# One signal for each unit of eight matmuls instead of one for each matmul, in a GNN kernel of gather passes

## The chip, the cores and the metric

The kernel runs on one core of a Trainium2 chip. Its five engines (TensorE or PE for matmuls, VectorE or DVE, ScalarE or ACT, GpSimd or POOL, SyncE or SP) run programs of their own and meet only at semaphores: an instruction can add to a semaphore when it is finished, and an engine can wait until a semaphore has reached a count. The metric is the time of one execution on the device in microseconds, the median of several timed runs. Beside these there is one execution under the hardware profiler, which is where all rows come from.

## The reference

Four graph networks run one after the other on 4096 nodes with 256 features and 65,536 edges (`src`, `dst`, sorted by `dst`), with a layer norm after each. All of them gather the rows of the source nodes, change them per edge, and add them up by destination node:

```
# layer of the first network, five times
emsg = relu(h_in[src] + edge_attr @ We[l] + be[l])
agg  = segment_sum(emsg, dst)
h    = mlp(h_in + agg) ... + h_in
# second: x[src] * edge_weight, segment_sum
# third:  attention; segment_max over dst of the scores, then
#         segment_sum of exp(score - max) * h[src]
# fourth: h[src] * norm, segment_sum, three times
```

`dst` is the floor of 4096 times the square of a uniform number. Of the 32 blocks of 128 nodes block b therefore ends at about the share sqrt((b+1)/32) of the edges: the first blocks have many edges each, the last about a thousand.

## The kernel before

There are eleven passes over the edges. Nine are made by `edge_pass`: five of kind MESSAGE (first network), one WEIGHTED (second), three PLAIN (fourth). `max_pass` finds the segment maximum, `attend_pass` does the attention sum and isn't touched. Between them stand node phases of dense matmuls.

A pass goes over 64 **octets** of eight tiles of 128 edges (U = 8). For each tile POOL issues one indirect DMA (L262), which gathers 128 rows into a slot of `ring`. The ring holds four octets (OB = 4): POOL begins octet h when PE has given octet h-4 free (`octet_free`) and ACT has copied its indices (`idx_ready`).

The sum by destination is a matmul. For an octet and a block of 128 destination nodes, a **unit**, DVE writes eight 128x128 one-hot matrices into `S` (`one_hots`, L235, two instructions of four matrices each, here called g0 and g1), and PE multiplies the eight of them with the eight ring tiles and adds up in `psA` (L331). An octet has as many units as blocks that its edges touch: one or two. With 32 blocks cut into 64 octets this makes 95 units in a pass; 31 octets have two, 7 of them in the first half of the pass, 24 in the second, and 14 of these among the last 16 octets.

`S` and `psA` exist once. In one unit DVE writes g0, which waits for the first four matmuls of the unit before (`onehot_used`, `c + 4 * g + 4`), then waits for all eight of them, adds `psA` to `AGG` (L373, `unit_added`), and writes g1. PE waits for `unit_added` before the first matmul and for `onehot_ready` before the first and the fifth. At the end of an octet's units PE reads the next count of units from `span_row`, which costs its sequencer a load and some register work.

MESSAGE passes have edge features besides. `encode` (L301) makes eight small bf16 matmuls for the next octet into `psE`, two at a time, each pair behind the DVE additions that have read the pair's bank (`pre_added`). DVE adds `psE` to the gathered rows (L388), ACT applies the relu (L347, `message`). PE does at each octet: encode for the next octet, then the load of the count, then the units. The stacked features come in by a DMA of SP, which waits until `encoded` counts the whole octet.

The max pass takes two octets at a time, a **group** of 16 gathers (L428). PE turns the scores (L440, L441, then `scoresT`), DVE scans them, PE turns them back, and the units follow (L457, 128x9), with `merge_last` (L492, L495 and on) in the place of the sum. POOL may begin group n+2 when `scoresT` has counted group n.

Of the kernel before, what the change touches and what calls it, by code (L numbers as in the profile page):

```python
# [22 lines left out]
U = 8  # L23
NO = NT // U
OB = 4
# [15 lines left out]
def build(nc, x, src, dst, edge_attr, edge_weight, vn_emb0, We, be, W1, b1, W2, b2, bn_g, bn_b, bn_m, bn_v,  # L41
# [3 lines left out]
    with ctx:  # L45
# [35 lines left out]
        we_stk = sb("we_stk", [P, D], BF16)  # L81
# [45 lines left out]
        picks = sb("picks", [P, MT, HEADS + 1])  # L127
# [16 lines left out]
        octet_free = sem("octet_free")  # L144
# [121 lines left out]
        def edge_pass(kind, k, l=0, loads=None, first_work=None, first_dve=None):  # L266
            with nc.Block() as block:
# [20 lines left out]
                @block.tensor  # L288
                def _(pe):
                    if first_work:  # L290
                        first_work[0](pe)
                    def encode(i, ob):

                        o = NO * l + OB * i + ob

                        pe.wait_ge(stk_in[ob], 16 * (NG * l + i + 1))
                        for u in range(U):
                            if u % 2 == 0:

                                pe.wait_ge(pre_added, U * o + u + 2)  # L300
                            nc.tensor.matmul(psE[:, D * u:D * u + D], stk[:, ob, P * u:P * u + P],  # L301
                                             we_stk[:, :], start=True, stop=True).then_inc(encoded, 1)

                    if kind == MESSAGE:
                        encode(0, 0)
                    with pe.Fori(0, NG) as i:
                        for ob in range(OB):
                            h = OB * i + ob
                            if kind == MESSAGE:

                                if ob < OB - 1:
                                    encode(i, ob + 1)
                                else:
                                    with pe.If(i < NG - 1):
                                        encode(i + 1, 0)
                            cnt = pe.value_load(span_row[0:1, bass.ds(2 * h + 1, 1)], min_val=1, max_val=NB)

                            def unit(_, first):
                                c = pe.snap(npe)

                                pe.wait_ge(unit_added, c + 2 * U)
                                for u in range(U):
                                    q = U * ob + u
                                    if first:
                                        if kind in (MESSAGE, WEIGHTED):
                                            pe.wait_ge(message, NT * k + U * h + u + 1)
                                        else:
                                            pe.wait_ge(gathered[q], 16 * (NG * k + i + 1))
                                    if u % 4 == 0:
                                        pe.wait_ge(onehot_ready, c + u + 4)  # L330
                                    nc.tensor.matmul(psA[:, 0:D], S[:, u, :], ring[:, q, 0:D],  # L331
                                                     start=(u == 0), stop=(u == U - 1)).then_inc(onehot_used, 1)
                                pe.reg_add(npe, npe, U)

                            units(pe, None, cnt, unit)
                            pe.drain().then_inc(octet_free, 1)

                @block.scalar
                def _(act):
# [16 lines left out]
                @block.vector  # L356
                def _(dve):
                    nc.vector.memset(AGG[:, :], 0.0)

                    nc.vector.memset(psA[:, 0:D], 0.0)  # L360
                    dve.reg_mov(last_blk, 0)
                    dve.drain()
                    if first_work:
                        first_work[2](dve)
                    if first_dve:
                        first_dve(dve)

                    def add_sums():

                        b = nc.s_assert_within(dve.snap(last_blk), 0, NB - 1,  # L370
                                               skip_runtime_bounds_check_because="a unit's block")
                        a = AGG[:, bass.ds(b * AW, D)]
                        return nc.vector.tensor_tensor(a, a, psA[:, 0:D], ALU.add)  # L373

                    with dve.Fori(0, NG) as i:
                        for ob in range(OB):
                            h = OB * i + ob
                            o = NO * l + h
                            lo, cnt = span_of(dve, h)

                            def messages():
                                for u in range(U):
                                    q = U * ob + u
                                    dve.wait_ge(gathered[q], 16 * (NG * k + i + 1))
                                    if u % 2 == 0:

                                        dve.wait_ge(encoded, U * o + u + 2 + OB * U)
                                    nc.vector.tensor_tensor(ring[:, q, 0:D], ring[:, q, 0:D],  # L388
                                                            psE[:, D * u:D * u + D], ALU.add).then_inc(pre_added, 1)

                            def unit(blk, first):
                                c = dve.snap(nd)
                                if first and kind == MESSAGE:
                                    messages()
                                one_hots(dve, h, blk, c, 0)

                                dve.wait_ge(onehot_used, c + U)
                                dve.wait_ge(unit_added, c + U)
                                add_sums().then_inc(unit_added, U)
                                one_hots(dve, h, blk, c, 1)  # L400
                                dve.reg_mov(last_blk, blk)
                                dve.reg_add(nd, nd, U)

                            units(dve, lo, cnt, unit)
                    c = dve.snap(nd)
                    dve.wait_ge(onehot_used, c + U)
                    dve.wait_ge(unit_added, c + U)
                    add_sums()
# [7 lines left out]
        def max_pass(k):  # L416
            with nc.Block() as block:
# [14 lines left out]
                @block.tensor  # L432
                def _(pe):
                    with pe.Fori(0, NG) as i:
                        for g in range(GR):
                            n = GR * i + g
                            for q in range(MT * g, MT * g + MT):
                                pe.wait_ge(gathered[q], 16 * (NG * k + i + 1))
                            pe.wait_ge(d16_ready, n + 1)
                            nc.tensor.transpose(psE[:, 0:P], gs[:, P * g:P * g + P], ident[:, :])  # L440
                            nc.tensor.transpose(psE[:, 512:512 + P], d16[:, :], ident[:, :]).then_inc(scoresT, 1)  # L441
                            pe.wait_ge(runs_ready, n + 1)
                            nc.tensor.transpose(psE[:, 1024:1024 + P], run[:, :], ident[:, :])
                            nc.tensor.transpose(psE[:, 1536:1536 + P], last[:, :], ident[:, :]).then_inc(runsT, 1)
                            pe.wait_ge(picks_ready, n + 1)
                            for half in range(2):
                                cnt = pe.value_load(span_row[0:1, bass.ds(2 * (2 * n + half) + 1, 1)],
                                                    min_val=1, max_val=NB)

                                def unit(_, first):  # L450
                                    c = pe.snap(npe)

                                    pe.wait_ge(unit_added, c + 2 * U)
                                    for u in range(U):
                                        if u % 4 == 0:
                                            pe.wait_ge(onehot_ready, c + u + 4)
                                        nc.tensor.matmul(psA[:, (HEADS + 1) * u:(HEADS + 1) * (u + 1)], S[:, u, :],  # L457
                                                         picks[:, U * half + u, :], start=True, stop=True
                                                         ).then_inc(onehot_used, 1)
                                    pe.reg_add(npe, npe, U)  # L460

                                units(pe, None, cnt, unit)
                                pe.drain().then_inc(octet_free, 1)

                @block.scalar
                def _(act):
# [1310 lines left out]
```

## Time and profile before

| | us |
|---|---|
| median of three timed runs | 9055.8 |
| lowest and highest of them | 9051.29, 9059.39 |
| the profiled execution, first to last instruction | 11096.4 |
| PE busy in it | 6221.1 (56%) |
| POOL busy in it | 5936.1 (53%) |
| DVE busy in it | 4228.8 (38%) |

The profiled execution took 2040.6 us more than the median of the timed ones, so its rows can't be added up to the time without asking which of them are there only under the profiler.
### The profile page before, as it was taken

All of it is one profiled execution on the core that took longest, in us unless ns stands there. A gap on an engine that the chain in (4) does not pass through costs nothing. (4 is left out here: it accounts for less than half of the span.)

```text
span 11096.4 us, 128036 instructions
## 1 busy us (share of the span) xinstructions
PE 6221.1 (56%) x27247; PEld 4898.8 (44%) x27248; DVE 4228.8 (38%) x9200; ACT 1828.6 (16%) x5238; POOL 5936.1 (53%) x5947
## 2 busy tenths in 40 slices
PE   3557655855575566557456434445663555456454
PEld 2445544634464455446344323434452344344343
DVE  5344444443443444434122723344453223124123
ACT  3222222222122222213332100001110000000000
POOL 2654465365536545652665365545545655655665
PEclk9789888978887888889788755567876788778787
DMA  4332333133323323332322000022222222222222
GB/s 148 106 97 79 93 102 90 56 115 99 89 67 106 94 77 92 104 91 67 90 83 72 19 3 2 2 55 72 72 55 73 85 78 77 85 76 72 85 87 71
DMA packets 424174, 855.04 MB, mean 77 GB/s; under 512 B 142497, under 2 KB 206754, under 8 KB 424098
## 3 DMA queue, kind: packets, MB, share of 16 engines
q0 software_dynamic: 263184, 679.84, 21.6%
q1 hardware_dynamic: 160914, 174.39, 5.2%
q8 instruction: 23, 0.38, 0.0%
q14 instruction: 53, 0.43, 0.0%
HBM read 790.64 MB, written 63.18 MB: 77 GB/s over the span
## 5 line engine op out<-in xcount | busy, mean ns | idle before, releaser
L262 POOL DMA_INDIRECT ring<-node_table,idx x4608 | 4557.0, 989 | 3214.9 <-issue 1615.9
L331 PE MATMUL psAT<-ring,S 128*128 128x256 f32 x13680 | 3792.2, 439 | 2375.5 <-DVE AGG L373 1330.1
L331 PEld LDWEIGHTS psAT<-ring,S 128*128 128x128 f32 x13680 | 2973.7, 223 | 3158.7 <-issue 1702.0
L235 DVE SCALAR_TENSOR_TENSOR S<-iota,block_start,dst_f 128x512 f32<-128x512 f32 x1900 | 1423.6, 749 | 3122.1 <-remote 1598.4
L347 ACT ACTIVATE ring<-ring 128x256 f32<-128x256 f32 x2560 | 885.8, 416 | 3282.4 <-DVE ring L388 2302.8
L388 DVE TENSOR_TENSOR ring<-ring,psE 128x256 f32<-128x256 f32 x2560 | 888.0, 416 | 399.5 <-remote 214.9
L373 DVE TENSOR_TENSOR AGG<-AGG,psAT 128x256 f32 x864 | 363.6, 421 | 1624.6 <-remote 1005.5
L301 PE MATMUL psE<-we_stk,stk 128*128 128x256 bf16 x2560 | 420.8, 318 | 963.6 <-issue 883.8
L262 POOL DMA_INDIRECT ring<-att_table,idx x512 | 513.3, 1003 | 491.4 <-issue 228.1
L301 PEld LDWEIGHTS psE<-we_stk,stk 128*128 128x128 bf16 x2560 | 254.8, 110 | 1147.6 <-issue 997.8
L428 POOL DMA_INDIRECT gs<-score_table,idx x512 | 508.9, 994 | 370.9 <-PE psE L441 214.8
L246 ACT COPY idx<-src_i 128x8 int32 x704 | 138.7, 197 | 3299.6 <-DMA ring<-node_table,idx 2352.7
L457 PE MATMUL psAT<-picks,S 128*128 128x9 f32 x1520 | 340.0, 363 | 309.5 <-DVE cand L495 197.0
L457 PEld LDWEIGHTS psAT<-picks,S 128*128 128x128 f32 x1520 | 331.4, 330 | 327.9 <-issue 201.5
L1428 POOL TENSOR_TENSOR tab<-H,be_row 128x256 f32<-128x256 f32 x128 | 105.9, 827 | 500.3 <-DVE H L1425 500.3
L351 ACT ACTIVATE ring<-ring,weight 128x256 f32<-128x256 f32 x512 | 259.0, 507 | 526.6 <-DMA ring<-node_table,idx 477.7
L952 PE MATMUL psE<-tT,w_sb 128*128 128x128 f32 x2560 | 315.3, 277 | 0.9 <-ACT tT L981 0.8
L952 PEld LDWEIGHTS psE<-tT,w_sb 128*128 128x128 f32 x2560 | 301.7, 193 | 2.4 <-ACT tT L981 2.1
L965 PE MATMUL psE<-w_sb,hT 128*128 128x256 f32 x1280 | 301.9, 379 | 0.0
L965 PEld LDWEIGHTS psE<-w_sb,hT 128*128 128x128 f32 x1280 | 231.4, 190 | 25.0
L990 ACT ACTIVATE hT<-psE,b_col 128x128 f32<-128x128 f32 x640 | 182.5, 368 | 228.8 <-PE psE L952 228.8
L939 PE MATMUL psAT<-ident,tin 128*128 128x128 f32 x320 | 67.2, 293 | 219.3 <-DVE tin L199 184.9
(268 smaller groups left out, 4359.6 us busy)
## 6 DMA issues: line engine op xcount, KB each, us to landing
stk<-stack_table SPq DMA_DIRECT2D x320, 256.0 KB
ring<-node_table,idx POOLq DMA_INDIRECT x4608
node_table<-tab SPq DMA_DIRECT2D x224, 128.0 KB, 1.7
stack_table<-stk SPq DMA_DIRECT2D x64, 256.0 KB, 2.0
gs<-score_table,idx POOLq DMA_INDIRECT x512
ring<-att_table,idx POOLq DMA_INDIRECT x512
w_sb<-in_L_gnn_W SPq DMA_DIRECT2D x10, 512.0 KB
att_table<-tab SPq DMA_DIRECT2D x32, 132.0 KB, 1.8
```

Source lines behind the costliest of these rows:

```text
L235: nc.vector.scalar_tensor_tensor(S[:, 4 * g:4 * g + 4, :], iota[:, :].unsqueeze(1).to_broadcast([P, 4, P]), block_start[:, bass.ds(blk, 1) ...
L262: nc.gpsimd.indirect_dma_start(ring[:, q, 0:gw], None, table, bass.IndirectOffsetOnAxis(ap=idx[:, q:q + 1], axis=0)).then_inc(gathered[q], 16)
L301: nc.tensor.matmul(psE[:, D * u:D * u + D], stk[:, ob, P * u:P * u + P], we_stk[:, :], start=True, stop=True).then_inc(encoded, 1)
L331: nc.tensor.matmul(psA[:, 0:D], S[:, u, :], ring[:, q, 0:D], start=(u == 0), stop=(u == U - 1)).then_inc(onehot_used, 1)
L347: nc.scalar.activation(ring[:, q, 0:D], ring[:, q, 0:D], ACT.Relu).then_inc(message, 1)
L351: nc.scalar.activation(ring[:, q, 0:D], ring[:, q, 0:D], ACT.Copy, scale=weight[:, bass.ds(RING * i + q, 1)]).then_inc(message, 1)
L373: return nc.vector.tensor_tensor(a, a, psA[:, 0:D], ALU.add)
L388: nc.vector.tensor_tensor(ring[:, q, 0:D], ring[:, q, 0:D], psE[:, D * u:D * u + D], ALU.add).then_inc(pre_added, 1)
L428: nc.gpsimd.indirect_dma_start(gs[:, HEADS * q:HEADS * q + HEADS], None, score_table, bass.IndirectOffsetOnAxis(ap=idx[:, q:q + 1], axis=0 ...
L457: nc.tensor.matmul(psA[:, (HEADS + 1) * u:(HEADS + 1) * (u + 1)], S[:, u, :], picks[:, U * half + u, :], start=True, stop=True).then_inc(o ...
L952: ins = nc.tensor.matmul(psE[:, 512 * q + P * j:512 * q + P * j + P], w1_sb[:, f, P * j:P * j + P], tT[:, q, P * f:P * f + P], start=(f == ...
L965: ins = nc.tensor.matmul(result_of(q), a, w, start=(n == 0), stop=(n == len(terms) - 1))
```

## The change

The matmuls of `encode` (L301), of the units of `edge_pass` (L331) and of the units of `max_pass` (L457) lose their increments. After each eight of them PE executes a drain, which ends when all matmuls before it are finished and adds 8 to the same semaphore. The drain that signalled `octet_free` at the end of an octet becomes a plain increment. In `messages()` DVE waits once for all eight encodings, not pair by pair. The counts of all semaphores at the end of a unit are as before, and no instruction changes its place in an engine's program; the waits on DVE are the same text, but `onehot_used` now rises by eight at once where it rose one by one, so that the wait of g0 for "the first four of the unit before" is now a wait for all eight and the drain.

```
-                                             we_stk[:, :], start=True, stop=True).then_inc(encoded, 1)
+                                             we_stk[:, :], start=True, stop=True)
+                        pe.drain().then_inc(encoded, U)
...
-                                                     start=(u == 0), stop=(u == U - 1)).then_inc(onehot_used, 1)
+                                                     start=(u == 0), stop=(u == U - 1))
+                                pe.drain().then_inc(onehot_used, U)
                                 pe.reg_add(npe, npe, U)
 
                             units(pe, None, cnt, unit)
-                            pe.drain().then_inc(octet_free, 1)
+                            pe.sem_inc(octet_free, 1)
...
-                                    if u % 2 == 0:
-
-                                        dve.wait_ge(encoded, U * o + u + 2 + OB * U)
+                                    if u == 0:
+
+                                        dve.wait_ge(encoded, U * o + U + OB * U)
...
-                                                         picks[:, U * half + u, :], start=True, stop=True
-                                                         ).then_inc(onehot_used, 1)
+                                                         picks[:, U * half + u, :], start=True, stop=True)
+                                    pe.drain().then_inc(onehot_used, U)
                                     pe.reg_add(npe, npe, U)
 
                                 units(pe, None, cnt, unit)
-                                pe.drain().then_inc(octet_free, 1)
+                                pe.sem_inc(octet_free, 1)
```

## Rows read from the trace of the kernel before

**Rows 1.** The page: span, engines, the gather group (busy, mean ns | idle).
```profile
span 11096.4 us, 128036 instructions
...
PE 6221.1 (56%) x27247; PEld 4898.8 (44%) x27248; DVE 4228.8 (38%) x9200; ACT 1828.6 (16%) x5238; POOL 5936.1 (53%) x5947
...
L262 POOL DMA_INDIRECT ring<-node_table,idx x4608 | 4557.0, 989 | 3214.9 <-issue 1615.9
```

**Rows 2.** Waits on POOL (us in total, times, longest).
```profile
POOL ring L262 <- PEq L336: 1497.1, 314, 26.1
...
POOL ring L262 <- ACT idx L246: 291.7, 62, 16.9
POOL gs L428 <- PE psE L441: 214.8, 29, 14.3
...
POOL ring L262 <- PEq L707: 67.3, 15, 12.4
```

**Rows 3.** Stretches: a MESSAGE pass, the max pass, a PLAIN pass.
```profile
core 0: us, PE busy (x) PEld busy (x) DVE busy (x) ACT busy (x) POOL busy (x), PEclk, DMA share, GB/s
1195.30:2092.20 896.90, 522.47 (x2107) 397.50 (x2105) 369.21 (x826) 189.12 (x579) 504.21 (x512) 0.81 0.33 97
...
6383.40:7308.50 925.10, 383.90 (x1648) 349.86 (x1648) 306.57 (x894) 12.62 (x64) 508.92 (x512) 0.50 0.05 2
...
8425.90:9249.40 823.50, 424.66 (x1520) 331.80 (x1520) 181.53 (x288) 12.63 (x64) 503.19 (x512) 0.79 0.28 82
```

**Rows 4.** Timeline of a PLAIN pass, one unit held up (start us, us, ..., [idle <-releaser]).
```profile
9023.85 3.71 PE L331 MATMUL psAT<-ring,S 128*128 128x256 f32 x16 [1.69 <-issue]
...
9032.67 0.75 DVE L235 SCALAR_TENSOR_TENSOR S<-iota,block_start,dst_f 128x512 f32<-128x512 f32 x1 [8.84 <-remote]
...
9042.50 0.42 DVE L373 TENSOR_TENSOR AGG<-AGG,psAT 128x256 f32 x1 [9.07 <-remote]
```

**Rows 5.** Timeline, end of a PLAIN pass, all gathers landed: three units.
```profile
9231.40 3.72 PE L331 MATMUL psAT<-ring,S 128*128 128x256 f32 x16 [1.26 <-DVE S L235]
9233.55 0.75 DVE L235 SCALAR_TENSOR_TENSOR S<-iota,block_start,dst_f 128x512 f32<-128x512 f32 x1 [2.17 <-PE psAT L331]
9235.27 0.42 DVE L373 TENSOR_TENSOR AGG<-AGG,psAT 128x256 f32 x1 [0.97 <-PE psAT L331]
...
9235.83 3.72 PE L331 MATMUL psAT<-ring,S 128*128 128x256 f32 x16 [0.71 <-DVE AGG L373]
...
9240.77 3.72 PE L331 MATMUL psAT<-ring,S 128*128 128x256 f32 x16 [1.22 <-DVE AGG L373]
```

**Rows 6.** Timeline, matmuls of the same shape without signals, node phase.
```profile
9257.02 1.03 PE L965 MATMUL psE<-wb_sb,tT 128*128 128x256 f32 x4
```

**Rows 7.** Timeline, a MESSAGE pass: one octet of two units, undisturbed.
```profile
4086.18 1.04 PE L301 MATMUL psE<-we_stk,stk 128*128 128x256 bf16 x8 [0.61 <-issue]
...
4087.70 3.71 PE L331 MATMUL psAT<-ring,S 128*128 128x256 f32 x16 [0.48 <-issue]
...
4092.14 3.72 PE L331 MATMUL psAT<-ring,S 128*128 128x256 f32 x16 [0.72 <-issue]
...
4096.11 0.75 DVE L235 SCALAR_TENSOR_TENSOR S<-iota,block_start,dst_f 128x512 f32<-128x512 f32 x1
```

**Rows 8.** Timeline, POOL's gathers in a PLAIN pass.
```profile
10613.12 0.94 POOL L262 DMA_INDIRECT ring<-node_table,idx  x1 [0.30 <-issue]
```

**Rows 9.** Timeline, the max pass: from one pair of transposes to the units.
```profile
7080.72 0.42 PE L441 MATMUL psE<-ident,d 128*128 128x128 f32 x1
...
7087.00 3.58 PE L457 MATMUL psAT<-picks,S 128*128 128x9 f32 x16 [2.57 <-DVE cand L495]
...
7091.27 3.58 PE L457 MATMUL psAT<-picks,S 128*128 128x9 f32 x16 [0.69 <-issue]
...
7106.33 3.58 PE L457 MATMUL psAT<-picks,S 128*128 128x9 f32 x16 [1.84 <-DVE cand L495]
...
7111.30 0.42 PE L441 MATMUL psE<-ident,d 128*128 128x128 f32 x1
```

## The prediction

> **What bounds the kernel now.** I read the page first. POOL and PE are both busy about half of the span, which decides nothing: 4608 gathers of 989 ns each stand on POOL with 3214.9 us of idle time around them [rows 1]. So next come the waits on POOL. It waited 1497.1 us for `octet_free` after PE's drain, 291.7 us for the indices from ACT, 214.8 us for the transposes of the max pass and 67.3 us for PE in the attention pass [rows 2], 2070.9 us in all. The profiled execution is 2040.6 us longer than the timed median. Take the four waits off the span, and 9025.5 us are left, 30.3 short of 9055.8.
>
> That is no accident of sums, I think, for the stall has a face. One unit's matmuls stand in the trace as issued from 9023.85 to 9027.56, but DVE, which needs the first four, starts g0 at 9032.67, and the sum, which needs eight, at 9042.50; both waits end in "remote" [rows 4]. At the end of a pass, with all gathers issued, the same unit's sum starts 0.15 us after its last matmul (9231.40 + 3.72 = 9235.12, then 9235.27) [rows 5]. So while gathers are in flight the signals of PE arrive late, up to 15 us for a unit. My reading is that the profiler makes most of this lateness, and that in a timed run POOL walks nearly freely through its gathers.
>
> A gather takes 0.94 us and stands 0.30 us after the one before [rows 8]; with the slower ones (mean 989 ns [rows 1]) an octet costs POOL about 10.1 us, a pass about 647 us. Against that stand the cycles of PE and DVE, undisturbed and at full clock:
> a PLAIN octet of two units: 9.4 us (9231.40 to 9240.77) [rows 5];
> a MESSAGE octet of two units: 10.3 us (4086.18, to 4092.14 + 3.72 for the last matmul, and 0.65 us until the next encode) [rows 7]; one of one unit: 10.3 - 4.4 = 5.9 us;
> a group of the max pass with four units: 4.27 us from unit to unit in an octet (7087.00 to 7091.27), about 4.7 over the octet's border, 5.9 us ahead of the first (from 7081.14) and 5.4 behind the last (7106.33 to 7111.72), 24.5 us [rows 9]; with three 20.2, with two 16.0. POOL needs 20.2 for its 16 gathers.
> POOL thus bounds the first half of every pass with room to spare, and PE with DVE are level with it at the end, where 14 of the last 16 octets have two units. In the max pass the eight groups of four units are bound by PE and DVE already.
>
> **The change part by part.**
> The signals taken away. Sixteen hardware matmuls (two for each fp32 one) with a signal on every second take 3.72 us [rows 5]; four of the same shape without any take 1.03 us [rows 6]. Their last ones hold 0.38 us each, which leaves (3.72 - 0.38)/15 = 0.22 and (1.03 - 0.38)/3 = 0.22 us a step. The signals cost PE nothing, and I book no gain.
> The Trainium skill, "TensorE: Matmul & The Clock Gate", section "The cost: per-tile semaphore tail", says that increments of packed matmuls queue up behind one another, with 26.3 ns each, and advises one increment on the last. By that page seven fewer are worth 0.18 us for a unit, an estimate, or 0.16 ms over 855 units if every one counted. Rows 5 show the sum 0.15 us after the last of eight matmuls, so here they don't queue.
>
> The drain of a unit, and g0. Today g0 runs under the second half of the unit: it starts 2.15 us into it (9233.55) [rows 5], and is done when the last matmul ends. Then come 0.15 us, the sum of 0.42, 0.14, and PE starts: 0.71 us idle. After the change g0 waits for the drain. DVE then does, one after another, about 0.25 us of signal and registers, g0 of 0.75, the sum, and PE starts 1.46 us after its last matmul: +0.75 us within an octet. At an octet's border PE idles 1.22 us today, since it loads the count after its drain [rows 5]; DVE's new chain of about 1.5 us is longer than that: +0.3 us. In MESSAGE passes DVE makes eight additions before g0, which starts at 4096.11, after the last matmul at 4095.86 [rows 7]: nothing there at an octet's border.
> The drain of encode. Today the load of the count goes under the small matmuls, and the unit starts 0.48 us behind them (4087.22 to 4087.70) [rows 7]. Behind a drain it costs what it costs at an octet's border, 1.22 us [rows 5]: +0.75 us in each MESSAGE octet. The trace has no drain right behind small matmuls; it can't cost less than 0, and no more than 1.22. The merged wait in `messages()` asks for encodings that were made an octet earlier: nothing.
> SP's wait on `encoded` gets its count up to 0.1 us later, with a ring of four behind it: nothing.
>
> The sum by stages, at full clock.
> PLAIN and WEIGHTED, four passes: an octet of two units rises to 9.4 + 0.75 + 0.3 = 10.4 us, of one unit to 5.3. The last 16 octets then take 14 x 10.4 + 2 x 5.3 = 156 us against POOL's 162. Covered; only the last octet stands behind the last gather, +1 us. 4 us together. Without the cover it would be 31 x 0.75 + 64 x 0.3 = 42 us a pass.
> MESSAGE, five passes: two units 10.3 + 1.5 = 11.8, one unit 6.7. The last 16 take 14 x 11.8 + 2 x 6.7 = 179 us against 162, where before they took 156: +17, and 2 for the last octet. But the granted clock is 0.81 over the pass [rows 3], so at 1.2 GHz in some units: then a unit takes about 6.8 us for 3.7, PE falls behind earlier, and more octets pay. I take 28 us a pass between 12 and the uncovered 33 x 0.75 + 31 x 1.5 = 71. 140 us.
> The max pass: within an octet +0.9, over its border +0.45 (the same chain with `merge_last` in place of the sum), so +2.3 for four units and +1.3 for three, which lifts these to 21.6, above POOL's 20.2. 8 x 2.3 + 15 x 1.3 = 38 us, less what the short groups give back: 25 us.
> Sum 4 + 140 + 25 = 169 us, rounded to 165. On the median of 9055.8: **9221 us**.
>
> **The rivals.**
> Faster: the late signals are partly real. Then one increment for eight would be late once and not eight times. For it: rows 4 are signals that come late, and the change has the right shape. Against it: the waits add up to the profiler's surplus within 30 us. What a timed run can still hold of them is those 30 us and the backlog at the end of each pass (some 15 us in each of eleven), at most 190 us; less 50 us of drains that remain, 140 gained, 8915 us. It decides where a timed run's signals lag by more than the 0.75 us that g0 now costs.
> Much slower: PE and DVE bound the timed passes too, since the clock stays at 1.2 GHz or the gathers go faster without the profiler. Then every octet pays: 5 x 71 + 4 x 42 + 38 = 561, 9617 us.
> No change: PE stays warm and the ring of four octets levels the end of a pass: only tails and the max pass, under 18 us, some 9065 us.
>
> **How the numbers follow.** A measurement of this kernel can tell 0.2%, 18 us, from no change. My forecast (9120 to 9400) has 0.62, much slower 0.13, no change 0.08, faster 0.17. Two in ten are left out with a range from 9000 to 9480: most of the faster case and the upper part of the much slower one. Slower 0.75, same 0.08, faster 0.17.
>
> **What would show it.** In the trace of after, g0 must start after the last matmul of the unit before, not in its middle; PE's idle time before a second unit goes from 0.71 to about 1.5 us, and between encode and unit from 0.48 to about 1.2. PLAIN passes must keep their gathers' pace. If the profiled span falls by hundreds of us while the timed median rises, the late signals were the profiler's; if both fall, I was wrong about them, and that is the step on which the sign rests.

## The result, and the profile after

| | before | after |
|---|---|---|
| median, us | 9057.59 (9051.29 to 9064.34, 4 runs) | 9298.51 (9276.52 to 9311.49, 4 runs) |
| ratio | | 1.0262, 95% interval 1.0249 to 1.0275 |
| profiled execution, span in us | 11096.4 | 9309.7 |
| mean granted clock of TensorE in it | | 0.846 |

The changed kernel is 241 us slower. The forecast was 165 us slower, 9221, in a range from 9000 to 9480. The sign and the two main gaps came as told; the size was too small.

The page of after, to be read beside [rows 1]:

```profile
span 9309.7 us, 128346 instructions
...
PE 6259.2 (67%) x27247; PEld 4721.9 (51%) x27248; DVE 4192.3 (45%) x9200; ACT 1865.5 (20%) x5238; POOL 5928.0 (64%) x5947
...
L262 POOL DMA_INDIRECT ring<-node_table,idx x4608 | 4543.7, 986 | 1879.5 <-issue 1674.9
L332 PE MATMUL psAT<-ring,S 128*128 128x256 f32 x13680 | 3924.2, 441 | 1514.8 <-DVE AGG L375 801.8
...
L235 DVE SCALAR_TENSOR_TENSOR S<-iota,block_start,dst_f 128x512 f32<-128x512 f32 x1900 | 1423.3, 749 | 3349.3 <-PEq L334 3159.5
...
L375 DVE TENSOR_TENSOR AGG<-AGG,psAT 128x256 f32 x864 | 357.3, 414 | 30.3 <-PEq L334 30.3
```

The busy times are those of before. New is who waits for whom: 3159.5 of DVE's some 5100 us of idle time stand ahead of g0 (L235), released by the drain at L334. The sum (L375), which used to wait for the last matmul, waits for next to nothing (30.3 us in all), as g0 has already waited for the drain that covers it. PE in turn waits 801.8 us for the sum.

The waits on POOL in after (engine, line, releaser: us in total, times, longest), beside [rows 2]:

```profile
POOL ring L262 <- PEq L338: 142.0, 81, 14.8
...
POOL ring L262 <- ACT idx L246: 79.7, 40, 5.4
...
POOL gs L430 <- PE psE L443: 33.6, 7, 6.9
```

They were 1497.1, 291.7 and 214.8 us. This is no gain of the change. The profiled execution of after is one of its timed ones (9311.49), so in this trace the span is the time. What made the trace of before 2040 us longer than its median is taken up below.

Timeline of after, end of a MESSAGE pass: encode, a first and a second unit. It answers to [rows 5] and [rows 7].

```profile
3473.99 1.05 PE L301 MATMUL psE<-we_stk,stk 128*128 128x256 bf16 x8 [0.76 <-issue]
...
3476.34 3.72 PE L332 MATMUL psAT<-ring,S 128*128 128x256 f32 x16 [1.31 <-issue]
...
3480.23 0.75 DVE L235 SCALAR_TENSOR_TENSOR S<-iota,block_start,dst_f 128x512 f32<-128x512 f32 x1 [4.99 <-PEq L334]
...
3480.90 0.42 DVE L375 TENSOR_TENSOR AGG<-AGG,psAT 128x256 f32 x1
...
3481.45 3.72 PE L332 MATMUL psAT<-ring,S 128*128 128x256 f32 x16 [1.39 <-DVE AGG L375]
```

The last matmul of the first unit ends at 3476.34 + 3.72 = 3480.06. g0 starts 0.17 us after it, then comes the sum, and PE starts 1.39 us after its last matmul (forecast 1.46, before 0.71). Encode ends at 3475.04 and the unit starts 1.30 us later (forecast 1.22, before 0.48). Over five MESSAGE passes the medians are 1.39 and 1.26 us. A third gap was booked as nothing: ahead of encode PE idles 0.76 us here, 0.78 in the median. Without the units' drains (e2_halves below) it is 0.25 at the least and 0.30 in the median.

### The profile page after: what moved, and what is told of

It is laid out like the page before. It is cut to its first block and busy times, and to the rows that moved or that the text cites. A ratio compares the mean times of both kernels' runs of the same rounds, so it can differ in the third digit from the quotient of the medians.

```text
span 9309.7 us, 128346 instructions
## 1 busy us (share of the span) xinstructions
PE 6259.2 (67%) x27247; PEld 4721.9 (51%) x27248; DVE 4192.3 (45%) x9200; ACT 1865.5 (20%) x5238; POOL 5928.0 (64%) x5947
## 5 line engine op out<-in xcount | busy, mean ns | idle before, releaser
L332 PE MATMUL psAT<-ring,S 128*128 128x256 f32 x13680 | 3924.2, 441 | 1514.8 <-DVE AGG L375 801.8
L332 PEld LDWEIGHTS psAT<-ring,S 128*128 128x128 f32 x13680 | 2867.5, 219 | 2535.6 <-DVE S L235 1407.9
L235 DVE SCALAR_TENSOR_TENSOR S<-iota,block_start,dst_f 128x512 f32<-128x512 f32 x1900 | 1423.3, 749 | 3349.3 <-PEq L334 3159.5
L349 ACT ACTIVATE ring<-ring 128x256 f32<-128x256 f32 x2560 | 925.5, 416 | 2459.9 <-DVE ring L390 2457.8
L390 DVE TENSOR_TENSOR ring<-ring,psE 128x256 f32<-128x256 f32 x2560 | 928.7, 415 | 501.2 <-DMA ring<-node_table,idx 446.6
L301 PE MATMUL psE<-we_stk,stk 128*128 128x256 bf16 x2560 | 359.6, 278 | 407.3 <-issue 202.4
L301 PEld LDWEIGHTS psE<-we_stk,stk 128*128 128x128 bf16 x2560 | 218.1, 99 | 585.2 <-issue 280.8
L375 DVE TENSOR_TENSOR AGG<-AGG,psAT 128x256 f32 x864 | 357.3, 414 | 30.3 <-PEq L334 30.3
```

The source lines that it names most:

```text
L235: nc.vector.scalar_tensor_tensor(S[:, 4 * g:4 * g + 4, :], iota[:, :].unsqueeze(1).to_broadcast([P, 4, P]), block_start[:, bass.ds(blk, 1) ...
L332: nc.tensor.matmul(psA[:, 0:D], S[:, u, :], ring[:, q, 0:D], start=(u == 0), stop=(u == U - 1))
L349: nc.scalar.activation(ring[:, q, 0:D], ring[:, q, 0:D], ACT.Relu).then_inc(message, 1)
L390: nc.vector.tensor_tensor(ring[:, q, 0:D], ring[:, q, 0:D], psE[:, D * u:D * u + D], ALU.add).then_inc(pre_added, 1)
```

## Experiments

The kernels fell on three chips. On chip A (e1 to e4) the kernel before takes 9057.6 us, as it does beside the result above; on chip C (those with a b, and r_after) it takes 9067.0. On chip B (e0, e6, e8, e9) the same kernel takes 11207.5 us, 24% more, timed and not only profiled. A ratio is always to the kernel before on the same chip.

**Which part of the change costs.** e1_last gives one signal for eight without a drain: the last matmul adds 8, in encode as in the units, and the drain ahead of `octet_free` is back. The edit of the units, against the changed kernel, shortened:

```
-  ... start=(u == 0), stop=(u == U - 1)).then_inc(onehot_used, 1)
+  ins = nc.tensor.matmul(...)
+  if u == U - 1:
+      ins.then_inc(onehot_used, U)
```

> Edit: no drains are added; only the last of eight matmuls carries a signal, of 8, in encode and in the units; the drain ahead of octet_free stays as before. What is left of the change is the late g0 alone. Theory (late g0 and the sequencer's work behind each drain share the cost): in a MESSAGE octet of two units 0.7 us of 2.1 stay, so some 10 us in each of five passes, 4 for the other edge passes, 20 for the max pass: about 9130 us. If the late g0 carried all of the cost: 9290, as the changed kernel. If the drains carried all: 9057, as before. Profiled span: close to the timed one, since seven signals of eight are gone.

Measured 9073.61, ratio 1.0021 [1.0012, 1.0031]. PE's idle time between two units is that of after, here at the end of a PLAIN pass:

```profile
8999.43 0.75 DVE L235 SCALAR_TENSOR_TENSOR S<-iota,block_start,dst_f 128x512 f32<-128x512 f32 x1 [3.35 <-PE psAT L332]
...
9000.65 3.72 PE L332 MATMUL psAT<-ring,S 128*128 128x256 f32 x16 [1.38 <-DVE AGG L376]
...
9004.52 0.42 DVE L376 TENSOR_TENSOR AGG<-AGG,psAT 128x256 f32 x1 [3.34 <-PE psAT L332]
```

So the late g0 (+0.67 us for each second unit) is real, and costs 16 us in all. By the traces of e1 and e2 these are the max pass (734.9 us from its first gather to its last merge, 718.5 in e2); the five MESSAGE passes are 0.9 us longer together and the other four 2.4 shorter. POOL covers it there. I had expected 9130, too much.

e2_halves is the same with a signal of 4 on the fourth and on the eighth matmul of a unit (`if u % 4 == 3: ins.then_inc(onehot_used, 4)`), which is all that DVE's waits look at.

> Edit: as the run with one signal on the last matmul, but the fourth and the eighth matmul of a unit carry a signal of 4 each, so that g0 can start in the middle of a unit again. Theory: within 0.2% of the kernel before, 9040 to 9075 us. Rival, that the single signals of before were late in timed runs too: this has two in place of eight and nothing else against it, so it would be 50 to 190 us faster than before, 8870 to 9000. Profiled span: theory and rival both below the 11096 us of before; by the theory 9050 to 9600.

Measured 9052.64, ratio 0.9994 [0.9984, 1.0004]. Six of eight signals of a unit are gone and seven of eight in encode, g0 is under the unit again (idle time 0.71 us), and the time is that of before. So nothing that can be measured is to be had from taking the signals away.

e3_encode_back is the changed kernel with encode and its waits as before.

```
                             nc.tensor.matmul(psE[:, D * u:D * u + D], stk[:, ob, P * u:P * u + P],
-                                             we_stk[:, :], start=True, stop=True)
-                        pe.drain().then_inc(encoded, U)
+                                             we_stk[:, :], start=True, stop=True).then_inc(encoded, 1)
```

> Edit: the changed kernel with encode as before (a signal on each small matmul, no drain, the wait by pairs). Theory: takes back 0.82 us (1.30 - 0.48 us of idle time of PE between encode and unit) in each MESSAGE octet that isn't covered by the gathers, some 16 to 20 octets in each of five passes: 65 to 85 us less than the changed kernel, about 9220. If encode's drain were covered: 9298. If it were the whole cost: 9100.

Measured 9129.4, ratio 1.0079 [1.0062, 1.0096]: the part of the units and of the max pass costs 72 us, and the rest of the 241, 169 us, comes with encode's drain. The expectation, 9220, was wrong: it gave encode's drain half of that.

e4_unread is the changed kernel with `.then_inc(unread, 1)` on each matmul of the units of the edge passes; nobody reads that semaphore.

> Edit: the changed kernel, and each of the eight matmuls of a unit of the edge passes also adds 1 to a semaphore that nobody waits for. Theory (a signal costs PE nothing in a timed run, the late signals of before were made by the profiler): timed as the changed kernel within 0.2%, 9280 to 9317; the profiled span goes back up by hundreds of us, towards 11000. Rival (single signals cost something in timed runs): timed above 9320. If the profiled span stays at 9310, it isn't the number of signals that the profiler makes late.

Measured 9311.48, ratio 1.0285 [1.0268, 1.0303], span 9302.1. Eight signals a unit are back over 855 units; the medians are 13 us apart, and as the intervals of 1.0285 and 1.0262 overlap, that isn't told from nothing. The profile is as short as without them, where the theory had it go back towards 11000. So on this chip the profiler doesn't make a kernel long by the number of its signals.

**Encode's part by itself.** e6 is the kernel before with the encode part of the change alone (drain, one wait for eight).

> Edit: the kernel before with encode's part of the change alone (no signal on the small matmuls, one drain behind each eight, the merged wait). Theory (the parts of the change don't add up: a MESSAGE octet of two units takes PE 9.9 us without the change and POOL 10.3 for its gathers, so 0.8 us more is half covered, while the same 0.8 on top of the other parts was worth 169 us): 9065 to 9100 us. If encode's drain costs 169 us wherever it stands: 9226.

On chip B: 11221.15, ratio 1.0015 [0.9987, 1.0044], undecided. On chip C:

> The kernel before with the encode part of the change alone: the eight encodings without signals, one drain that counts them, one wait of DVE for the eight; units as before. The same kernel as e6_encode_alone, tried again to see it where the kernel before takes 9.06 ms. There the change without this part lost 72 us and the whole change 241 to 254, so its share is 169 to 182 us as a difference. Theory (the drain of encode costs 0.77 us in each MESSAGE octet whatever the units do, and PE is behind the gathers only where its cycle is over POOL's 10.3 us): alone it makes a two-unit octet 10.7 us, which is little over POOL's pace, so it costs much less than its share in the whole: about 9100 us, ratio 1.003 to 1.007; idle time from encode to unit 1.25 us, between two units 0.7 us. Rival (the two drains add up, each with a price of its own): 9057 + 169 = 9226 us, ratio 1.019. Where the kernel before takes 11.2 ms, the same kernel gave 1.0015.

Measured 9077.89, ratio 1.0013 [1.0003, 1.0022]. The timeline has the gap that was forecast for after, 1.26 to 1.32 us between encode and unit:

```profile
1660.17 1.05 PE L301 MATMUL psE<-we_stk,stk 128*128 128x256 bf16 x8 [0.82 <-DVE ring L389]
1662.53 3.72 PE L332 MATMUL psAT<-ring,S 128*128 128x256 f32 x16 [1.32 <-issue]
1666.96 3.72 PE L332 MATMUL psAT<-ring,S 128*128 128x256 f32 x16 [0.71 <-DVE AGG L374]
1670.94 1.05 PE L301 MATMUL psE<-we_stk,stk 128*128 128x256 bf16 x8 [0.26 <-issue]
1673.24 3.72 PE L332 MATMUL psAT<-ring,S 128*128 128x256 f32 x16 [1.26 <-ACT ring L348]
```

From encode to encode that is 10.77 us, just over the 10.3 that POOL takes there for an octet. So the same drain costs 11 us alone and 169 us on top of the units' drains on chip A. On chip C it would be 145 if the units' part costs 72 us there too, which wasn't run. The parts don't add up, and what lies between them is POOL's pace, as the table further down bears out.

**What the encode drain exposes.** e8 moves the load of the count in the changed kernel ahead of encode.

```
+                            cnt = pe.value_load(span_row[0:1, bass.ds(2 * h + 1, 1)], min_val=1, max_val=NB)
                             (encode, its drain)
-                            cnt = pe.value_load(span_row[0:1, bass.ds(2 * h + 1, 1)], min_val=1, max_val=NB)
```

> Edit: the changed kernel, with PE's load of the count of units moved ahead of encode, so that encode's drain stays and the sequencer's work behind it goes. Theory (the drain itself is nearly free, what stands behind it costs): PE idles about 0.5 us between encode and unit, not 1.27, and the time is within 30 us of the kernel with encode as before, 9110 to 9160. If the drain itself costs: 9280 to 9310.

> The changed kernel with one instruction group moved: PE reads the next count of units before it starts the encodings and not behind their drain. All signals and drains are those of the changed kernel. Theory (what the encode drain costs is the load and the register work of PE's sequencer that it no longer lets run under the small matmuls): the idle time from encode to unit goes from 1.27 back to about 0.5 us, the two-unit octet from 11.8 to about 11.0 us, and of the 169 us that the encode part costs 120 or more come back: 9130 to 9180 us, ratio 1.008 to 1.013 on the chip where the kernel before takes 9.06 ms. Rival (the drain and the later signal to DVE cost it, whatever the sequencer does afterwards): 9290 to 9310 us, ratio 1.026 to 1.028. A load that now lies open after the units costs up to 0.5 us in each octet of all passes; it would show as a longer border before encode.

Chip B: 11358.75, ratio 1.0107 [1.0075, 1.0138]. Chip C: 9312.57, ratio 1.0268 [1.0251, 1.0285], beside 1.0247 [1.0228, 1.0267] for the changed kernel there. Nothing came back, and my theory fell in its consequence. The timeline tells why:

```profile
1707.39 3.72 PE L332 MATMUL psAT<-ring,S 128*128 128x256 f32 x16 [1.39 <-DVE AGG L375]
1712.50 1.04 PE L301 MATMUL psE<-we_stk,stk 128*128 128x256 bf16 x8 [1.39 <-issue]
1714.01 5.40 PE L332 MATMUL psAT<-ring,S 128*128 128x256 f32 x16 [0.47 <-issue]
1720.81 3.71 PE L332 MATMUL psAT<-ring,S 128*128 128x256 f32 x16 [1.39 <-DVE AGG L375]
1726.28 1.04 PE L301 MATMUL psE<-we_stk,stk 128*128 128x256 bf16 x8 [1.75 <-issue]
```

Between encode and unit the idle time did fall from 1.26 to 0.48 us, so it is the load and the register work that the drain lays open. But the load now stands behind the unit's drain, and the gap ahead of encode grew from 0.78 to 1.58 us (medians). Before the change this work ran while small matmuls were in the array. With a drain on both sides of encode there is no such place ahead of it or behind its drain. Between the eight matmuls and their drain there would be one; that version wasn't tried.

**The clock.** In the second halves of the MESSAGE passes PE is behind the gathers, and the granted clock differs from kernel to kernel. The windows are the second half of the second MESSAGE pass; columns as in [rows 3]. e2_halves, which stands for before on a fast chip; after; e3_encode_back:

```profile
1348.60:1678.50 329.90, 256.27 (x1136) 194.83 (x1135) 187.71 (x421) 98.36 (x288) 252.15 (x256) 0.94 0.42 124
```

```profile
1391.30:1742.20 350.90, 254.51 (x1078) 196.45 (x1079) 173.76 (x401) 88.06 (x272) 250.77 (x256) 0.91 0.40 117
```

```profile
1355.60:1686.70 331.10, 247.32 (x1136) 190.64 (x1136) 184.70 (x421) 96.10 (x288) 253.37 (x256) 0.97 0.41 124
```

Each window ends with the last gather. The same 256 gathers, 250.8 to 253.4 us of work for POOL, take 21.0 us more in after than in e2, and the granted clock is 0.91. A unit whose time falls in part on the lower level takes 5.40 us at a clock of 0.68 (1714.01 above), where it takes 3.72 at the full one (1707.39). In the second half of this pass 19 units are so slow in after, 12 in r_after, 8 in e2, 4 in e3. Is the low clock a companion of the loss or a cause? e9 adds work to the changed kernel where PE idled: behind encode's drain eight more small matmuls into a bank that nobody reads there.

```
                         pe.drain().then_inc(encoded, U)
+                        if fill:
+                            for u in range(U):
+                                nc.tensor.matmul(psV[:, 0:D], ident_b[:, :], we_stk[:, :], start=True, stop=True)
```

> Edit: the changed kernel, and behind each drain of encode eight small matmuls of constants into a bank that the pass doesn't use; they fill the 1.27 us in which PE idles and the sequencer loads the count. Theory (part of the cost is the granted clock, 0.90 in the second half of a MESSAGE pass against 0.97 with encode as before): the clock of that half goes to 0.95 or more, and the kernel with more work is faster than the changed one by 40 to 90 us, about 9230. Rival (the clock is a mere consequence of PE's waiting and costs nothing): 9298 or more, up to 9370.

> The changed kernel with work added: behind the drain of each encode (not of the first in a pass) PE makes eight more small matmuls of the same size into a bank that nobody reads in these passes, so that it is busy where it idled for the load of the count. Rival on the clock (the lower granted clock of the second half of MESSAGE passes, 0.90 to 0.91 against 0.97, comes from PE's idle gaps, and the clock is most of the loss): the clock goes back to 0.96 and more, and the time falls by 40 us or more below the changed kernel's, under 9260 us. Theory (the loss is the longer cycle, and the lower clock follows from it or adds only a part): eight matmuls take 0.8 to 1.0 us where 1.27 us were idle, the cycle of a two-unit octet gets no shorter, and the time is 9290 to 9350 us, with the clock at most 0.02 higher.

> The changed kernel itself, beside the three others on the same chip, as their reference. Where the kernel before takes 9.06 ms: 9298 us, ratio 1.026. Where the kernel before takes 11.2 ms (the signals of PE come late there while gathers are in flight, by up to 20 us and more): if late signals can be saved by sending one for eight, as the rival of the prediction has it, the ratio is under 1.00; if the drains cost there too what they cost elsewhere, 1.005 to 1.02.

Chip C: e9b 9193.53, ratio 1.0139 [1.0122, 1.0156]; r_after 9283.9, ratio 1.0247 [1.0228, 1.0267]. With 2520 matmuls more, whose results are thrown away, the kernel is 90 us faster than r_after. This is what the theory of e9 and the rival of e9b said, and the theory of e9b didn't. The page's mean clock went from 0.845 to 0.861, and in the same half pass, windows and timeline of e9b:

```profile
1371.30:1704.60 333.30, 264.04 (x1346) 201.07 (x1347) 180.99 (x415) 93.61 (x282) 255.63 (x256) 0.99 0.42 123
```

```profile
1665.69 1.04 PE L301 MATMUL psE<-we_stk,stk 128*128 128x256 bf16 x8 [0.62 <-issue]
1666.82 1.04 PE L306 MATMUL psV<-we_stk,ident_b 128*128 128x256 bf16 x8
1667.99 3.71 PE L335 MATMUL psAT<-ring,S 128*128 128x256 f32 x16
1673.09 3.71 PE L335 MATMUL psAT<-ring,S 128*128 128x256 f32 x16 [1.39 <-DVE AGG L378]
1677.78 1.04 PE L301 MATMUL psE<-we_stk,stk 128*128 128x256 bf16 x8 [0.97 <-issue]
```

The octet is no shorter: 12.09 us from encode to encode, 12.0 in the median of a pass's last sixteen octets and 11.7 in the shortest tenth, which is what after has when its clock is full. Only the slow units are gone: of some 58 units in a second half none takes over 4.5 us in the first four MESSAGE passes of e9b, 12 to 14 do in r_after and 19 or 20 in after. What they take beyond 3.72 us adds up to under 1, to 19 to 23 and to 32 to 35 us a pass. The Trainium skill, "TensorE: Matmul & The Clock Gate", section "A second HAM failure mode: psum-queue depth-cycling", tells of another kernel in which short idle times between groups of matmuls make the clock go back and forth between its levels. The trace agrees: 0.91 with three gaps of 0.78, 1.26 and 1.39 us in an octet of two units, 0.99 with the middle one filled. The gaps alone don't tell the clock, though: e2_halves has the shortest of them (0.30, 0.57 and 0.71 us in the median), and e3_encode_back, with two longer ones, has the higher clock (0.97 against 0.94).

Means over the first four MESSAGE passes, from the first gather to the last sum, worked out from the traces:

| | a pass, us | clock, second half | two-unit octet, shortest tenth, us |
|---|---|---|---|
| e2_halves | 684.7 | 0.94 | 9.9 |
| e6b_encode_alone | 685.8 | 0.95 | 10.7 |
| e3_encode_back | 687.3 | 0.97 | 11.0 |
| e9b_busy | 702.1 | 0.995 | 11.7 |
| r_after | 717.7 | 0.94 | 11.7 |
| after | 729.8 | 0.91 | 11.7 |

Up to 11.0 us the octet is nearly free. That the ring of four octets and the shorter octets of one unit take it up is my reading; no run changed either. At 11.7 it costs 17 us a pass with the clock full, and 33 to 45 with the clock that after gets. The last two rows are one kernel in two executions, on chips C and A: more clock, less time.

**The chip on which everything is late.** e0_before is the kernel before, unchanged.

> Edit: none, the kernel before once more, for a second trace of it. If its long profiled span (11096 us) belongs to the kernel and its signals, this one is near 11000 too. If it belongs to that one execution, this one is near 9057.

Measured 11211.05 under the profiler, median 11207.52 without: no surplus. Its waits on POOL:

```profile
POOL ring L262 <- PEq L336: 1526.6, 329, 26.4
...
POOL ring L262 <- ACT idx L246: 306.7, 61, 16.6
POOL gs L428 <- PE psE L441: 272.5, 29, 14.7
...
POOL ring L262 <- PEq L707: 70.0, 21, 12.7
```

These are close to [rows 2], and the timeline has the late signals of [rows 4], here 8.0 us from the unit's last matmul (8917.05 + 5.37) to g0:

```profile
8917.05 5.37 PE L331 MATMUL psAT<-ring,S 128*128 128x256 f32 x16 [5.82 <-issue]
8930.46 0.75 DVE L235 SCALAR_TENSOR_TENSOR S<-iota,block_start,dst_f 128x512 f32<-128x512 f32 x1 [13.81 <-remote]
```

On the chips A and C the same kernel is timed at 9057.6 and 9067.0 us. It wasn't profiled there, but its nearest relative, e2_halves, has a span of 9054.1 us with the same profiler, a median of 9052.64, and this for the drain at the octet's end:

```profile
POOL ring L262 <- PEq L339: 56.2, 12, 14.2
```

So the late signals belong to the chip or to its state at the time, not to the profiler. Why that chip is late stays open. e9_busy gave 11409.59 there, ratio 1.0168 [1.0122, 1.0213], no better than e8_load_first with 1.0107 [1.0075, 1.0138]. The eight small matmuls did little for the clock (0.797 against 0.783); that idle times as long as the 5.82 us above are the reason is argued only. The changed kernel itself wasn't measured on chip B. Its two close relatives lose 1 to 2% there, and POOL's waits of the four kinds above, 2175.8 us in e0, add up to 2203.5 in e8_load_first and 2345.4 in e9_busy: one signal for eight leaves the late ones where they are.

No version that ran beats the kernel before by more than can be measured; e2_halves is level with it.

## Why the prediction came out as it did

**The waits of POOL in the trace of before.** The step was right in what it was used for, and wrong in its cause. A timed run at 9056 us has next to none of the 2070.9 us (the trace of e2_halves has 87 us of these waits), and the sum could be made on POOL's free walk. But "the profiler makes most of this lateness" is refuted by e0 on chip B, where profiled and timed runs are equally long. That the trace of before comes from such a chip, and its timed runs from another, is inferred from the likeness of the two traces. The fit within 30 us was evidence that the waits are absent from the timed runs, and none on why. With the wrong cause I would have forecast the same for a chip on which they are present.

**The signals are free.** Right: a unit takes 3.72 us with eight signals [rows 5] and with none (after), and e2_halves and e4_unread agree. The tail of the Trainium skill, "TensorE: Matmul & The Clock Gate", section "The cost: per-tile semaphore tail", doesn't show for these full-size fp32 matmuls: by its 26.3 ns some 0.16 ms were to be had, an estimate, and e2, which takes six of eight away and adds no drain, is at 0.9994.

**The drain of a unit.** Right within 0.07 us: 1.39 for 1.46. (The terms that the prediction names for it, 0.25, 0.75, 0.42 and 0.14, add up to 1.56; 1.46 is 0.71 + 0.75.) A drain's signal arrives 0.17 us after the last matmul, a matmul's own 0.15. What a drain costs more than a signal on the last matmul is e3 less e1, 56 us by the medians (encode's signals differ between the two as well). By the traces 13 us of it are in the MESSAGE passes, where the gap ahead of encode is 0.80 against 0.29 us, 12 in the max pass and 26 in the WEIGHTED and PLAIN passes.

**"Nothing there at an octet's border" in MESSAGE passes.** Wrong. I looked at DVE's side alone, where the additions hide g0. On PE's side encode comes next. It used to be issued while the unit's matmuls ran, and now stands behind the drain with the registers' work and the branch: 0.30 to 0.78 us. That the forecast length of a two-unit octet, 11.8 us, came out at 11.7 is luck: it was 10.3 + 1.5, and is 9.9 + 1.8. The 10.3 had 0.65 us ahead of the next encode, read from the slow trace, where a fast chip has some 0.26 (e6b's rows above), and this made up for the rise that was booked as nothing.

**The drain of encode.** The size was right, 1.26 for 1.22, from the row of a drain at an octet's border. That it costs nothing where the cycle stays at POOL's pace is e6b.

**The sums.** The terms of the prediction add up to 169; "rounded to 165" is no rounding, and nothing hangs on it. Measured are the profiled spans of after and of e2_halves, 255.6 us apart:

| | forecast | measured |
|---|---|---|
| MESSAGE, five passes | 140 | 218 |
| max pass | 25 | 28 |
| WEIGHTED and PLAIN, four passes | 4 | 16 |
| attention pass and outside | 0 | -7 |

The term that was mis-sized is the MESSAGE pass, 28 us taken and 37 to 48 measured. My sum at full clock (17 + 2 us) is borne out by e9b: 17 us more than e2_halves with a clock of 0.995. What I put on top for the clock, 9 us, was too little. In e2_halves the clock of the second half is 0.94 as in r_after, but there PE has slack, and a slow unit hides behind the gathers. In after PE has hardly any, and most of what such a unit takes longer is on the path; in the run of after there were also more of them (0.91). That is worth 16 us a pass by r_after against e9b and 28 by after, on another chip, against e9b. Of the loss about 90 us are the clock's by the medians of chip C. The prediction's 6.8 us for a unit was too long for most of them: the typical slow unit takes 5.40. Why one execution of after gets 0.94 and another 0.91 stays open.

The max pass: a group of three units takes 21.97 us, one of four 27.42 (forecast 21.6 and 26.8), read from one transpose to the next:

```profile
5895.52 0.47 PE L442 MATMUL psE<-ident,gs 128*128 128x128 f32 x1 [1.99 <-issue]
...
5917.49 0.47 PE L442 MATMUL psE<-ident,gs 128*128 128x128 f32 x1 [1.64 <-issue]
...
5944.91 0.47 PE L442 MATMUL psE<-ident,gs 128*128 128x128 f32 x1 [1.96 <-issue]
```

The PLAIN passes keep their pace but for 3 to 6 us each, and most of that shows in POOL's gathers (12 of 15 us in the three). The windows of the last PLAIN pass, e2_halves and then after:

```profile
8315.10:8981.90 666.80, 475.34 (x1489) 308.18 (x1490) 188.89 (x285) 12.44 (x63) 511.13 (x512) 0.83 0.34 101
```

```profile
8564.90:9237.70 672.80, 450.33 (x1495) 305.37 (x1496) 180.35 (x285) 12.44 (x63) 517.09 (x512) 0.86 0.35 100
```

The pass is 6.0 us longer, and the gathers themselves, POOL's busy time, are 5.96 us longer.

**The rivals.** "Faster" is out: what it needed, late signals in timed runs, isn't there on chips A and C, and on B such versions lose too. "Much slower" (9617) is out, since the first halves of the passes and the PLAIN passes are covered. "No change" is what encode's part is by itself, nearly (1.0013); the units' part (1.0079) is already clear of noise, and the two together are far from it.

## What to carry to other kernels

Price a drain by the sequencer work that it pushes out from under the matmuls, on each side of it, and not by the wait for its signal alone. Add up the cycle of the engine with all parts of a change and hold it against the pace of the bounding engine, as parts that are free one by one aren't together once that line is passed. Where TensorE becomes the late engine, units at the lower clock that were hidden are on the path; a few matmuls of no use in its idle gaps are a cheap test of what they cost.

## What the runs showed of the hardware that was not expected

- Useless work can pay: 2520 small matmuls in gaps of 1.26 us lifted the granted clock of the second halves of MESSAGE passes from 0.94 to 0.995 and took 90 us off 9284.
- The same kernel takes 9057.6, 9067.0 and 11207.5 us on three chips. On the third PE's signals come late while gathers are in flight (8 us in the rows above; POOL waits up to 26.4 us for PE's drain), and its timed runs are as long as the profiled one.
- A gather takes 0.945 us on POOL when no one-hot matrices are written at the time, and 1.04 us on the mean, 1.47 at the most, when it overlaps such a write (e2_halves, the second PLAIN pass: 271 and 241 gathers). Timeline of e2_halves:

```profile
8104.57 0.95 POOL L262 DMA_INDIRECT ring<-node_table,idx  x1 [0.30 <-issue]
...
8105.58 0.75 DVE L235 SCALAR_TENSOR_TENSOR S<-iota,block_start,dst_f 128x512 f32<-128x512 f32 x1 [2.13 <-PE psAT L332]
8105.82 1.33 POOL L262 DMA_INDIRECT ring<-node_table,idx  x1 [0.30 <-issue]
```

The second of these gathers starts while DVE writes `S`, and takes 1.33 us. In after, which has both writes of a unit close together, such gathers take 1.08 to 1.09 us on the mean in the PLAIN passes (one of 9.15 us left out). But that they are close together doesn't explain what these passes lose: e1_last has them so too, with 1.03 to 1.05 us, and its three PLAIN passes take 2008.1 us, against 2014.3 in e2_halves and 2029.5 in after. No run took the writes away, so that they slow a gather is argued and not shown, and the few us of the PLAIN passes stay open.
